# Cross attention on one core: the order of the opening's matmuls, V kept in fp32 through DRAM, and the place of the row maximum

## What is computed

```python
scale = HEAD_DIM ** (-0.5)                       # 16 heads of 64
a = _layer_norm(audio_kv, ln_gamma, ln_beta)     # 8 x 64 keys, 1024 wide
Q = (hidden_states @ Wq.T)                       # 8 x 1024 rows, 1024 wide
K = (a @ Wk.T)
V = (a @ Wv.T)
scores = einsum('bhtd,bhsd->bhts', Q, K) * scale # masked
attn = softmax(scores, axis=-1)
out = einsum('bhts,bhsd->bhtd', attn, V)
return hidden_states + tanh(gate) * (out @ Wo.T)
```

## Time and profile before

| | us |
|---|---|
| median of 3 runs | 1492.25 |
| all runs | 1492.04, 1492.25, 1496.14 |
| the profiled execution | 1494.74 |
| its span in the trace | 1493.0 |
| PE busy in it | 1467.3 (98%) |
| DVE, ACT, POOL busy | 1163.7, 894.1, 537.7 |

### The profile page before, as it was taken

How to read it: one execution, slowest core, us unless ns; L and a number is a source line. 1 busy time by engine, 2 the same in 40 slices (tenths; PEclk the granted TensorE clock), 3 DMA queues, 4 the chain that set the end, 5 groups by cost and what they waited for, 6 DMA issues and landing times.

```text
span 1493.0 us, 20136 instructions
## 1 busy us (share of the span) xinstructions
PE 1467.3 (98%) x6624; PEld 1194.6 (80%) x6624; DVE 1163.7 (78%) x1349; ACT 894.1 (60%) x1894; POOL 537.7 (36%) x364
## 2 busy tenths in 40 slices
PE   6999999999999999999999999999999999999999
PEld 5666788888888888888787788888888888888887
DVE  6445788787878787979866788888888888888843
ACT  4556655455555555555776667766777776677521
POOL 5334000000000000000124566677766667776640
PEclk9999999999999999999999999999999999999999
DMA  7699865657575747474579988788887878888732
GB/s 281 215 376 391 292 216 198 216 199 231 183 233 174 242 159 257 142 253 132 168 254 328 297 250 243 235 248 244 265 267 238 234 242 248 242 265 266 212 118 84
DMA packets 303144, 348.51 MB, mean 233 GB/s; under 512 B 35648, under 2 KB 177088, under 8 KB 303040
## 3 DMA queue, kind: packets, MB, share of 16 engines
q1 hardware_dynamic: 287808, 332.54, 70.2%
q10 hardware_dynamic: 15232, 14.68, 2.8%
HBM read 198.26 MB, written 145.75 MB: 230 GB/s over the span
## 4 chain that ended last, share of the span: by engine, by line
PE 89%; DVE 3%; DMA 3%; issue 1%; SPq 1%; ACT 1%; POOL 1%; DVEq 0%; ACTq 0%; POOLq 0%
PE banks L1194 29%; PE banks L1196 29%; PE banks L1195 29%; PE banks L1223 3%; DMA m_scratch<-m_stage 1%; DMA probs<-s_scratch 1%; DVE parts L983 1%; DMA b_raw<-m_stage 1%; DVE a_ring L977 1%; PE banks L1262 0%; SPq L475 0%; DVE b_raw L1003 0%; DMA b_raw<-m_scratch 0%; PE banks L1188 0%; DVE a_sum L1047 0%
## 5 line engine op out<-in xcount | busy, mean ns | idle before, releaser
L1194 PE MATMUL banks<-parts,a_ring 128*128 128x512 f32 x1792 | 699.5, 390 | 4.3 <-DVE a_ring L977 3.5
L1196 PE MATMUL banks<-parts,a_ring 128*128 128x512 f32 x1792 | 697.5, 389 | 0.0
L1195 PE MATMUL banks<-parts,a_ring 128*128 128x512 f32 x1792 | 697.2, 389 | 0.0
L1194 PEld LDWEIGHTS banks<-parts,a_ring 128*128 128x128 f32 x1792 | 336.4, 188 | 76.2 <-DVE a_ring L977 6.1
L1196 PEld LDWEIGHTS banks<-parts,a_ring 128*128 128x128 f32 x1792 | 336.3, 188 | 70.2
L1195 PEld LDWEIGHTS banks<-parts,a_ring 128*128 128x128 f32 x1792 | 336.4, 188 | 69.3
L977 DVE TENSOR_TENSOR a_ring<-a_sum,a_ring 128x1024 fp32r<-128x1024 f32 x128 | 227.1, 1774 | 76.6 <-ACT a_ring L748 76.5
L748 ACT CAST a_ring<-a_sum 128x1024 fp32r<-128x1024 f32 x128 | 134.3, 1049 | 233.8 <-PE banks L1196 205.3
L1072 DVE TENSOR_TENSOR c_out<-banks,c_out 128x1024 f32<-128x1024 f32 x158 | 192.0, 1215 | 100.4 <-PE banks L1196 98.6
L818 ACT ACTIVATE probs<-probs,neg_max 128x64 f32<-128x64 f32 x1024 | 258.6, 337 | 1.2 <-DVE neg_max L1086 1.2
L657 POOL TENSOR_TENSOR probs<-probs,row_rec 128x512 f32<-128x512 f32 x128 | 134.6, 1052 | 241.3 <-DVE row_rec L1095 241.3
(11 more groups left out here) (77 smaller groups left out, 1350.8 us busy)
## 6 DMA issues: line engine op xcount, KB each, us to landing
xq<-x_t SPq DMA_DIRECT2D x32, 1024.0 KB, 6.2
s_scratch<-c_out SPq DMA_DIRECT2D x64, 512.0 KB, 3.1
probs<-s_scratch SPq DMA_DIRECT2D x128, 256.0 KB, 4.2
c_out<-x SPq DMA_DIRECT2D x63, 512.0 KB, 5.5
out<-c_out SPq DMA_DIRECT2D x63, 512.0 KB, 4.2
b_raw<-m_scratch SPq DMA_DIRECT2D x29, 1024.0 KB, 6.8
m_scratch<-m_stage SPq DMA_DIRECT2D x16, 1792.0 KB, 14.0
p_scratch<-p_turned SPq DMA_DIRECT2D x448, 64.0 KB, 2.6
```

Of the source, the lines that this page charges most:

```text
L1194: pe.matmul(to, wl, mh, start=first, stop=False, skip_group_check=joined)
L1195: pe.matmul(to, wh, ml, start=False, stop=False, skip_group_check=joined)
L1196: return pe.matmul(to, wh, mh, start=False, stop=last, skip_group_check=joined)
```

## The change

Three things are changed together.

1. **The order of the opening.** `TURNS` is gone. `OPS` now has two M operations, then two of K or V (after the third and the sixth such group one more), and PE does each operation whole, in that order. On ACT, the weight split that used to stand ahead of the copies of every M operation stands behind them for the second M operation of a group.
2. **V.** ACT writes V once, in fp32 (`copy_v`); DVE does nothing for V in the opening. The store is 1 MB for each half instead of 2 MB, and `load_v` brings half as many bytes, into the place where lo will stand (`v_raw` lies over `v_diag`, plane 1). The split now happens in the main loop: for each batch and each `four`, in the slot three before the first use, ACT makes hi (`split_v_hi`, two instructions on 64 rows x 256) and DVE lo (`split_v_lo`, two more, which wait for both of ACT's). They stand last in ACT's and in DVE's slot. `values` waits for DVE's.
3. **The row maximum** stands behind `split_p_lo` and `turn_blocks` in DVE's slot; only the new `split_v_lo` is behind it.

```diff
-        TURNS = [[("K", 0, c)] for c in range(NC)] + [[("K", 1, 0)], [("K", 1, 1)]]
-        for i in range(2 * NC):
-            TURNS.append([("M", i // NC, i % NC), others.pop(0)])
-            if i in (5, 11):
-                TURNS.append([others.pop(0)])
-        TURNS += [[op] for op in others]
-        OPS = [op for turn in TURNS for op in turn]
+        OPS = [("K", 0, c) for c in range(NC)] + [("K", 1, 0), ("K", 1, 1)]
+        for i in range(0, 2 * NC, 2):
+            OPS += [("M", i // NC, i % NC), ("M", i // NC, i % NC + 1), others.pop(0), others.pop(0)]
+            if i in (4, 10):
+                OPS.append(others.pop(0))
+        OPS += others
...
+        def v_split(z):
+
+            return [(b, four) for b in range(B) for four in range(2) if values_at(16 * b + 4 * four) // 4 - 3 == z]
...
-                    src = v_scr[b * S:(b + 1) * S, 4 * four:4 * four + 4, :, rr].rearrange("s g t e -> s (g t) e")
-                    to = v_diag[rr, 4 * four:4 * four + 4, :, rr].rearrange("s g t e -> s (g t) e")
-                    sp.dma_start(to.bitcast(F32), src).then_inc(v_in[four], 16)
+                    src = v_scr[b * S:(b + 1) * S, HD * four:HD * (four + 1)].rearrange("s (g e) -> s g e", g=4)
+                    sp.dma_start(v_raw[rr, 4 * four:4 * four + 4, 1, rr], src[:, :, rr]).then_inc(v_in[four], 16)
...
+            def split_v_hi(b, four):
+                act.wait_ge(v_in[four], 32 * (b + 1))
+                for h in range(2):
+                    rr = slice(h * HEAD, (h + 1) * HEAD)
+                    nc.scalar.copy(v_diag[rr, 4 * four:4 * four + 4, 0, rr], v_raw[rr, 4 * four:4 * four + 4, 1, rr]
+                                   ).then_inc(v_hi_made, 1)
...
-                if t + LEAD < ITEMS:
+                second = kind == "M" and OPS[t - 1][0] == "M"
+                if t + LEAD < ITEMS and not second:
                     split_weight_hi(t + LEAD)
                 if kind == "M":
                     for p in range(4):
                         copy_m(NC * half + c, p)
                         if (half, c) == (1, 5) and p % 2 == 1:
                             split_b_hi(0, p // 2)
+                    if t + LEAD < ITEMS and second:
+                        split_weight_hi(t + LEAD)
...
+            def split_v_lo(b, four):
+                dve.wait_ge(v_hi_made, 4 * b + 2 * four + 2)
+                for h in range(2):
+                    rr = slice(h * HEAD, (h + 1) * HEAD)
+                    hi, lo = (v_diag[rr, 4 * four:4 * four + 4, t, rr] for t in range(2))
+                    nc.vector.tensor_tensor(lo, v_raw[rr, 4 * four:4 * four + 4, 1, rr], hi.bitcast(F32), ALU.subtract
+                                            ).then_inc(v_lo_made, 1)
...
                     for u in units(soft_slot, z - SUM):
                         sum_rows(u)
-                    for u in units(soft_slot, z - MAX):
-                        row_max(u)
                     for u in units(split_slot, z):
                         if u < ON_PE:
                             split_p_lo(u)
                     for u in units(soft_slot, z - TURN):
                         if u >= ON_PE:
                             turn_blocks(u)
+                    for u in units(soft_slot, z - MAX):
+                        row_max(u)
+                    for b, four in v_split(z):
+                        split_v_lo(b, four)
...
-            first = 0
-            for turn in TURNS:
-                for quarter in range(4):
-                    for w in range(first, first + len(turn)):
-                        tile = {"K": k_tile, "M": m_pair, "V": v_tile}[OPS[w][0]]
...
+            for w in range(ITEMS):
+                pe.wait_ge(w_lo_made, w + 1)
                 for quarter in range(4):
+                    {"K": k_tile, "M": m_pair, "V": v_tile}[OPS[w][0]](w, quarter)
```

More of the change, by code:

```diff
@@ L177, in xattn_kernel @@
         v_in = sems("v_in", 2)
+        v_hi_made = sem("v_hi_made")
+        v_lo_made = sem("v_lo_made")
         s_in = sems("s_in", PROBS)
@@ L424, in store_v @@
             def store_v(half):
-                sp.wait_ge(v_lo_made, CT * (half + 1))
-                to = v_scr[:, HC * half:HC * (half + 1)].rearrange("(i p) g t e -> p i (g t e)", p=P)
-                sp.dma_start(to, v_out[half][:].rearrange("p i g t e -> p i (g t e)").bitcast(F32)
+                sp.wait_ge(v_made, CT * (half + 1))
+                sp.dma_start(v_scr[:, HD * half:HD * (half + 1)].rearrange("(i p) e -> p i e", p=P), v_out[half][:]
                              ).then_inc(v_stored[half], 16)
@@ L716, in copy_m, with copy_v @@
                                ).then_inc(m_copied_a, 1)
-            def copy_v_hi(half, i):
+            def copy_v(half, i):
                 act.wait_ge(v_done, CT * half + i + 1)
@@ L723, in copy_v_hi @@
                     act.wait_ge(v_done, 2 * CT)
-                nc.scalar.activation(v_out[half][:, i, :, 0, :], banks[:, 4 + i, :].rearrange("p (g e) -> p g e", g=HC), ACT.Copy,
-                                     scale=v_scale[:, i:i + 1]).then_inc(v_hi_made, 1)
+                nc.scalar.activation(v_out[half][:, i, :], banks[:, 4 + i, :], ACT.Copy, scale=v_scale[:, i:i + 1]
+                                     ).then_inc(v_made, 1)
             for i in range(CT):
@@ L883, in _ @@
                         exponential(u)
+                    for b, four in v_split(z):
+                        split_v_hi(b, four)
         @block.vector
@@ L965, in copy_m @@
                                       ).then_inc(m_copied_b, 1)
[L967 to L972, removed]
             def split_a_lo(s):
@@ L1121, in _ @@
                     split_k_lo(half)
-                elif c == NC - 1 and half == 0:
-                    for i in range(CT):
-                        split_v_lo(0, i)
             for q in range(2, 4):
@@ L1133, in _ @@
             sum_a(0, P5)
-            for i in range(2):
-                split_v_lo(1, i)
             for s in range(STEPS):
@@ L1141, in _ @@
                     split_a_lo(s + 1)
-                if s == 0:
-                    for i in range(2, CT):
-                        split_v_lo(1, i)
                 if n < ROUNDS:
@@ L1239, in v_tile @@
                     m.then_inc(kv_used, 1)
-            first = 0
-            for turn in TURNS:
+            for w in range(ITEMS):
+                pe.wait_ge(w_lo_made, w + 1)
                 for quarter in range(4):
-                    for w in range(first, first + len(turn)):
-                        tile = {"K": k_tile, "M": m_pair, "V": v_tile}[OPS[w][0]]
-                        if len(turn) == 1:
-                            if quarter == 0:
-                                pe.wait_ge(w_lo_made, w + 1)
-                            tile(w, quarter)
-                        elif quarter % 2 == 0:
-                            if quarter == 0:
-                                pe.wait_ge(w_lo_made, w + 1)
-                            tile(w, quarter)
-                            tile(w, quarter + 1)
-                first += len(turn)
+                    {"K": k_tile, "M": m_pair, "V": v_tile}[OPS[w][0]](w, quarter)
             def transpose_p(u):
```

18 lines of the change are left out of this document (9 added, 9 removed).

## The result

The changed kernel takes 1511.53 us, the median of 4 runs (1511.07 to 1513.01), beside 1493.65 us (1492.04 to 1496.14) for the kernel before on the same chip: a ratio of 1.012, 95% interval 1.0101 to 1.0138. The prediction was 1498.5, with a range up to 1505. It had the right sign and a third of the size, and the time lies above the range.

The account below looks back on a forecast made before the run. It took PE as the bound almost everywhere. Opening order and stores +3.3, V in the opening -1.6, row maximum -2.5 and V's main-loop split +7.0 gave +6.2 on 1492.25: 1498.5 us, range 1486.5 to 1505.

Follow-up runs that it names:

- e9: The changed kernel with VectorE's second subtraction of each V split on the first's partitions (0 to 63) instead of 64 to 127; 1502.91 us, ratio 1.0058.

## What to carry to other kernels

Before a two-operand SBUF instruction of VectorE goes beside a busy GpSimd, read from the trace what GpSimd runs then and how much margin the next operand has: contention of 3 us cost 0.2 us where the operand was due one step later, and 2.24 us where the margin was 0.84. Let such an instruction begin before GpSimd's long one and not behind another engine's result; one step earlier in ScalarE's order took all six gaps away. And a short stall of TensorE can cost nearly twice its length (2.24 us and 1.75 behind it).

## What was not expected of the hardware

- **The clock behind short gaps.** In the 14 profiles the main loop has 26 gaps between matmuls of 1.9 to 2.5 us (start to start, less 0.23). Behind 11 of them the granted clock was at the 1.2 GHz level for 3.41 us, which cost 1.6 to 1.8 us where it can be read by itself. Behind 37 gaps of 1.07 to 1.84 us, the six of 1.45 in e9 among them, it never was. Ahead of each of the six gaps in the changed kernel PE had been busy for 87 us or more. What picks 11 of 26 stays open, and with it over a quarter of the loss is measured but not explained.
- **32 ns.** The two VectorE instructions on different halves of the partitions did not overlap in any of 16 pairs; here that gave GpSimd the next turn and made 2.24 us out of 1.45, six times.
- **GpSimd pays too.** Its 128x512 subtraction took 2.27 us where it came second and 1.47 where VectorE's first subtraction was just ending; alone it takes 1.3 (its 2.27 of before, was such a case).
